# Cross-attention and mixture of experts: the order of the work between the last tanh and the first expert

## The reference

```
a    = x + xattn(layernorm(x), context)
       h   = tanh(text[t] + feature[f] + b)        for all 1024 x 77 pairs, 256 wide
       rho = h . w ; att = softmax(rho) ; text summed by att
       two tanh gates scale and shift the token
xn2  = layernorm(a)
prob = softmax(xn2 @ gate)                         8 experts
top  = the 512 of 4096 tokens with the largest prob, for each expert
out  = a + shared FFN(xn2) + scatter_add(top, prob * expert FFN(xn2[top]))
       FFN: 256 -> 1024, gelu, 1024 -> 256; each expert has weights of its own
```

## Time and profile before

| | |
|---|---|
| median of 3 runs | 893.86 us (893.48 to 893.88) |
| span of the profiled execution, first to last instruction | 892.1 us |
| TensorE busy | 801.3 us (90%) |
| ScalarE busy | 767.8 us (86%) |
| VectorE busy | 708.7 us (79%) |
| GpSimd busy | 307.6 us (34%) |

### The profile page before, as it was taken

The page is one execution under the profiler, slowest core; times in us unless marked ns, Lnnn a source line. Parts: engine busy times, 40 slices in busy tenths (PEclk is TensorE's granted clock), DMA queues, the critical chain, the costliest instruction groups (busy, mean ns, idle before and its releaser), DMA issues.

```text
span 892.1 us, 14125 instructions
## 1 busy us (share of the span) xinstructions
PE 801.3 (90%) x5385; PEld 472.7 (53%) x5385; DVE 708.7 (79%) x1405; ACT 767.8 (86%) x601; POOL 307.6 (34%) x537
## 2 busy tenths in 40 slices
PE   7975679569998999999999999999988999999996
PEld 5321123124443444445454455545766899999986
DVE  5899889898989689988878995894887877676641
ACT  3989999999999999999999999997753677676672
POOL 3310540615543007674002740052203145555424
PEclk9899999999999999999999999999999999999998
DMA  8000000000001000200000010002202365544513
GB/s 267 19 1 0 1 1 1 1 24 15 10 9 40 1 1 25 71 2 1 24 1 1 25 48 1 24 1 89 77 24 78 98 181 142 136 106 132 137 20 41
DMA packets 32406, 41.82 MB, mean 47 GB/s; under 512 B 2365, under 2 KB 29011, under 8 KB 32339
## 3 DMA queue, kind: packets, MB, share of 16 engines
q1 hardware_dynamic: 26083, 32.49, 10.9%
q0 software_dynamic: 6144, 8.39, 5.7%
q10 hardware_dynamic: 112, 0.04, 0.0%
HBM read 28.33 MB, written 12.58 MB: 46 GB/s over the span
## 4 chain that ended last, share of the span: by engine, by line
PE 39%; ACT 38%; issue 11%; DVE 9%; POOL 1%; DMA 0%; POOLq 0%; ACTq 0%; DVEq 0%
ACT z L995 31%; PE bank L914 10%; PE bank L937 9%; PE bank L787 7%; DVE z L1372 4%; PE bank L829 3%; PE bank L844 3%; ACT z L991 2%; ACT u L1038 2%; PE bank L763 2%; PE bank L715 1%; PE bank L952 1%; PE bank L817 1%; ACT L1038 1%; PE bank L888 1%
## 5 line engine op out<-in xcount | busy, mean ns | idle before, releaser
L995 ACT ACTIVATE z<-z 128x4096 f32<-128x4096 f32 (+5 forms) x157 | 520.9, 3364 | 4.6 <-DVE z L1372 4.4
L1372 DVE TENSOR_SCALAR z<-feat,txt_bias 128x1024 f32<-128x1024 f32 (+1 forms) x722 | 421.9, 656 | 36.5 <-PE bank L787 35.6
L787 PE MATMUL bank<-z,window 128*32 128x512 f32 x2464 | 304.9, 604 | 64.0 <-ACT z L995 62.5
L787 PEld LDWEIGHTS bank<-z,window 128*32 128x32 f32 x2464 | 70.0, 110 | 249.7 <-issue 134.1
L844 PE MATMUL bank<-ws_sb,u 128*128 128x256 f32 x512 | 126.3, 387 | 5.6 <-ACT u L1038 5.6
L844 PEld LDWEIGHTS bank<-ws_sb,u 128*128 128x128 f32 x512 | 92.2, 189 | 41.1 <-issue 19.8
L829 PE MATMUL bank<-tr,ws_s 128*128 128x512 f32 x384 | 107.9, 417 | 0.0
L914 PE MATMUL bank<-xg_s,w_s 128*128 128x512 f32 x384 | 99.5, 397 | 0.2 <-DVE xg_s L1672 0.2
L937 PEld LDWEIGHTS bank<-w_s,hid_s 128*128 128x128 f32 x672 | 86.3, 188 | 4.0
L937 PE MATMUL bank<-w_s,hid_s 128*128 128x256 f32 x672 | 88.2, 280 | 0.0
L1074 ACT ACTIVATE hid<-bank,vec 128x512 f32<-128x512 f32 x64 | 44.2, 690 | 49.3 <-PE bank L914 49.2
(11 more groups left out here) (264 smaller groups left out, 750.4 us busy)
## 6 DMA issues: line engine op xcount, KB each, us to landing
w_raw<-in_L_ffn_W_dram SPq DMA_DIRECT2D x16, 1024.0 KB, 5.6
x_ring<-in_x_dram SPq DMA_DIRECT2D x8, 512.0 KB, 7.9
xn_dram<-xn SPq DMA_DIRECT2D x8, 512.0 KB, 2.9
out_dram<-x_ring SPq DMA_DIRECT2D x8, 512.0 KB, 3.2
u<-in_L_ffn_Ws_dram SPq DMA_DIRECT2D x1, 1024.0 KB, 11.0
ws_sb<-in_L_ffn_Ws_dram SPq DMA_DIRECT2D x1, 1024.0 KB, 13.7
xg<-xn_dram,idx POOLq DMA_INDIRECT x32, 4.1
out_dram<-y,idx POOLq DMA_INDIRECT x32, 3.9
```

What stands on the lines that cost most here:

```text
L787: ins = e.matmul(sums[v][32 * r:32 * r + 32, :], window[:, c, 31 - k:63 - k], z[:, n % ZB, at_piece:at_piece + TOK], start=(v, r) not in b ...
L995: e.activation(part, part, ACT.Tanh).then_inc(signal(*step), 1)
L1372: ins = e.tensor_scalar(z[:, n % ZB, i * width:(i + 1) * width], feat_of(units, c), bias_of(units, t, c), None, ALU.add)
```

## The change

- **Sums ahead of FFN pieces.** In the last three blocks, `down` steps are taken out of the order and put behind the sums (`behind`), down(5,6) in two halves: the first behind `rho_out(7)`, the second behind `att_exp(7)`. Each of the last three blocks is summed by itself.
- **A gelu moved.** Of the four held gelus of unit 6, the first now stands ahead of `weigh(7)`, two behind the gates, and the fourth behind `logits_exp(7)`. `down_end(5,0)` moves to where `down_end(5,1)` was; `down_end(5,1)` and `store_out(5)` go behind the router.
- **The pieces' order and numbers.** down(6,0) and down(6,1) are interleaved so that bank 4 is used first; the two `down_end(6)` become two separate pieces.
- **First weights split on GpSimd.** A new step `split_first` does the copy and the subtract of each of the eight pieces on GpSimd, ahead of `masks` in its queue, behind `whole(7)`, which now stands in test 0. `split_hi` and `split_lo` of expert 0 go. The waits on them (`load_w1(1)`, `load_w2(1)`, `e_up`, `e_down`) turn to the new step.
- **VectorE idle in the first gathers.** `mark(1)` waits until gather 1 of the first four has landed (`FIRST_IN = 1`).
- **Around the first expert.** `mark_slots(1,3)`, `list(1,3)`, `fold(1)`, `folded(1)` and `gather(1)` come behind the turns of expert 0's rows, among its first steps; four filler pieces stand behind the turns.
- **Other banks.** Expert 0's gathered rows are turned into banks 0 and 1, and no more into 6 and 7.

The waits and banks of the steps follow in the code of each engine (`split_last`, `turned_bank`), which is left out here.

```diff
@@ -31,7 +31,7 @@
 AHEAD = 3
-TOGETHER, TOGETHER_FROM = 2, 93
+TOGETHER, TOGETHER_FROM, ALONE = 2, 93, 3
 BUSY = (20, 3, 5)
...
@@ -52,15 +52,17 @@
-TAIL_FILL = (7, 3)
-GELUS_BEFORE = 1
-TEST_FILL = (4, 4, 6, 4, 7, 3, 5, 5, 2, 3)
+TAIL_FILL = (4, 3)
+GELUS_BEFORE, GELUS_AFTER = 1, 3
+TEST_FILL = (5, 5, 6, 5, 7, 3, 5, 5, 3, 3)
 RANK_FILL = (1, 3, 6, 4)
-EXPERT_FILL = (23, 4, 0)
-SECOND_FILL = (8, 3, 2, 2, 9)
+SECOND_FILL = (8, 3, 3, 3)
+TURN_FILL = 2
 LIST_FILL = (0, 1, 0, 0)
 LAST_END = 1
+FIRST_IN = 1
+SPLIT_EARLY = 5
...
@@ -178,7 +180,7 @@
-            parts = (0, J // 2, J) if v == va - 1 and m == M - 1 else (0, J)
+            parts = (0, J // 2, J) if v == va - 1 and m >= M - 2 else (0, J)
             at_slots(n, FFN_PLACES, [[("up", v, m, 0, passes)], [("gelu", v, m)],
...
@@ -201,10 +203,14 @@
         summed.append(("rho", n))
-        if n < TOGETHER_FROM or n % TOGETHER == TOGETHER - 1 or n in unit_ends:
+        if LAST - ALONE <= n < LAST - 1:
+            steps = slots.pop(n, [])
+            behind += [step for step in steps if step[0] == "down"]
+            order += [step for step in steps if step[0] != "down"]
+        if n < TOGETHER_FROM or n >= LAST - ALONE or n % TOGETHER == TOGETHER - 1 or n in unit_ends:
             order += summed
             summed.clear()
-        if n < LAST - 1:
+        if n < LAST - ALONE:
             order += slots.pop(n, [])
...
@@ -224,12 +230,15 @@
-    lead = [step for steps in filler for step in steps]
-    filler = [piece for m in range(4) for piece in up(va, m)] + down(va, 0) + down(va, 1) + up(va, 4) + up(va, 5)
+    lead = behind + [step for steps in filler for step in steps]
+    filler = [piece for m in range(4) for piece in up(va, m)] + down(va, 0)[:2] + down(va, 1)[:2] + up(va, 4) + down(va, 0)[2:3]
+    filler += up(va, 5) + down(va, 0)[3:] + down(va, 1)[2:]
     for m in range(2, M):
     last_ffn = up(vb, 0) + [piece for m in range(1, M) for piece in up(vb, m) + down(vb, m - 1)] + down(vb, M - 1)
-    filler += last_ffn[:ENDS_BEHIND] + [down_ends(va)] + last_ffn[ENDS_BEHIND:]
+    ends = down_ends(va)
+    filler += last_ffn[:ENDS_BEHIND] + [ends[:1]] + last_ffn[ENDS_BEHIND + 2:ENDS_BEHIND + 4]
+    filler += last_ffn[ENDS_BEHIND:ENDS_BEHIND + 1] + [ends[1:]] + last_ffn[ENDS_BEHIND + 1:ENDS_BEHIND + 2] + last_ffn[ENDS_BEHIND + 4:]
...
@@ -244,18 +253,19 @@
-    first_split = [("split_hi", name, 0, h) for name in ("w1", "w2") for h in range(PIECES[0])]
+    first_split = [("split_first", name, h) for name in ("w1", "w2") for h in range(PIECES[0])]
     late = {step[1:3] for step in held}
-    order += [("logits_exp", va), ("router", va), *end[0], *(step for step in lead if step[0] == "up"), *end[1],
-              ("load_w1", 0), ("load_w2", 0), *end[2], ("att_exp", vb)]
-    order += [step for step in lead if step[0] == "down" and step[1:3] not in late]
+    downs = [step for step in lead if step[0] == "down" and step[1:3] not in late]
+    order += [("logits_exp", va), ("router", va), *end[0], *(step for step in lead if step[0] == "up"), downs.pop(0), *end[1],
+              ("load_w1", 0), ("load_w2", 0), *end[2], ("att_exp", vb), *downs]
     fill_chain(8)
     ends = [step for step in lead if step[0] in BY_VECTOR]
-    order += [*ends[:1], *held[:GELUS_BEFORE], *end[4], *end[5], *ends[1:], *end[6], *held[GELUS_BEFORE:]]
+    order += [*held[:GELUS_BEFORE], *end[4], *end[5], *ends[:1], *end[6], *held[GELUS_BEFORE:GELUS_AFTER]]
+    order += [*end[7], *end[9], *end[8], ("logits_exp", vb), *held[GELUS_AFTER:], ("y_shift_last", vb), ("router", vb),
+              ("values", NT - 2 * J, NT), *ends[1:]]
     held.clear()
-    order += [*end[7], *end[9], *end[8], ("logits_exp", vb), ("y_shift_last", vb), ("router", vb), ("values", NT - 2 * J, NT)]
     order += [step for step in lead if step[0] == "down" and step[1:3] in late]
...
@@ -270,7 +280,7 @@
         if k == 0:
-            order += reversed(end[10])
+            order += [*reversed(end[10]), *end[13], *first_split[:SPLIT_EARLY]]
         held.clear()
...
@@ -278,32 +288,25 @@
         order += steps
-    order += end[13]
-    high, low = [*first_split], [("split_lo", *step[1:]) for step in first_split]
+    order += first_split[SPLIT_EARLY:]
     fill(RANK_FILL[0])
-    order += [("masks",), high.pop(0), ("ranks",), ("rank_total",)]
+    order += [("masks",), ("ranks",), ("rank_total",)]
     fill(RANK_FILL[1])
-    order += [("offsets",), high.pop(0), ("ranked",)]
-    order.append(("slots_turn",))
+    order += [("offsets",), ("ranked",), ("slots_turn",)]
     fill(RANK_FILL[2])
-    order += [("slots",), high.pop(0)]
-    order.append(("mark", 0))
+    order += [("slots",), ("mark", 0)]
     fill(RANK_FILL[3])
     for q in range(4):
-        order += [("mark_slots", 0, q), ("list", 0, q), high.pop(0)]
+        order += [("mark_slots", 0, q), ("list", 0, q)]
         if q == 3:
         fill(LIST_FILL[q])
-    order += [*high, ("fold", 0), ("folded", 0), ("gather", 0)]
-    order += low[:PIECES[0]]
+    order += [("fold", 0), ("folded", 0), ("gather", 0)]
     fill(SECOND_FILL[0])
     order.append(("mark", 1))
-    for q in range(4):
+    for q in range(3):
         order += [("mark_slots", 1, q), ("list", 1, q)]
-        if q == 3:
-            order.append(("listed", 1))
         fill(SECOND_FILL[1 + q])
-    order += [("fold", 1), ("folded", 1), ("gather", 1)]
...
@@ -341,14 +344,14 @@
-    fill(max(0, len(filler) - sum(EXPERT_FILL)))
-    order += [*turn_gathered(0), *low[PIECES[0]:], ("load_w1", 1), ("load_w2", 1)]
-    for m in range(LAG):
+    order += [*turn_gathered(0), ("mark_slots", 1, 3), ("load_w1", 1), ("load_w2", 1)]
+    fill(TURN_FILL)
+    order += [("list", 1, 3), ("listed", 1), ("e_up", 0, 0), ("fold", 1), *up(0, 0)[1:3], ("folded", 1), ("gather", 1), *up(0, 0)[3:]]
+    for m in range(1, LAG):
         order += up(0, m)
+    fill(len(filler))
     for ex in range(E - 1):
         for m in range(M):
-            if ex == 0 and m < len(EXPERT_FILL):
-                fill(EXPERT_FILL[m])
             ahead = m + LAG
...
@@ -551,6 +554,9 @@
+        def turned_bank(ex, c):
+            return (MISC if ex else RHO)[c]
+
         EMPTIES = {
...
@@ -633,6 +639,9 @@
             return last_s[:, m - HC] if ex == E - 1 and m >= HC else hid_s[:, m % HC]
+
+        def split_last(name, ex):
+            return done("split_lo", name, ex, PIECES[1] - 1) if ex else done("split_first", name, PIECES[0] - 1)
...
@@ -1247,6 +1256,13 @@
                                     ALU.subtract).then_inc(signal(*step), 1)
+                elif kind == "split_first":
+                    name, h = args
+                    raw, parts = halves(name, 0, h)
+                    e.wait_ge(loaded[f"{name}_0"], 16)
+                    link(e.tensor_copy(parts[0], raw))
+                    e.wait_ge(pool_link, linked)
+                    e.tensor_tensor(parts[1], raw, parts[0].bitcast(F32), ALU.subtract).then_inc(signal(*step), 1)
                 elif kind == "gather":
...
@@ -1626,6 +1642,8 @@
                     ex, = args
+                    if ex == 1:
+                        e.wait_ge(first_gathered[FIRST_IN], 16)
                     link(e.tensor_tensor(in_tile[:], slot_a[:, :, ex:ex + 1].broadcast_to([P, NT, A]),
```

More of the change, by code:

```diff
@@ L190, in add @@
         order.append(("add", n))
-    summed, unit_ends = [], {*ends_at.values()}
+    summed, unit_ends, behind = [], {*ends_at.values()}, []
     for n in range(AHEAD - 1):
@@ L560, in xattn_moe_kernel @@
             "offsets": lambda: TOTAL, "slots": lambda: MISC[0], "listed": lambda ex: LIST,
-            "folded": lambda ex: SLOTS, "g_lo": lambda ex, c: MISC[c], "e_gelu": lambda ex, m: UP[m % 2],
+            "folded": lambda ex: SLOTS, "g_lo": lambda ex, c: turned_bank(ex, c), "e_gelu": lambda ex, m: UP[m % 2],
         }
@@ L685, in _ @@
                     else:
-                        e.wait_ge(*done("split_lo", "w1", ex - 1, PIECES[ex > 1] - 1))
+                        e.wait_ge(*split_last("w1", ex - 1))
                     if ex == 1:
@@ L693, in _ @@
                     if ex > 0:
-                        e.wait_ge(*done("split_lo", "w2", ex - 1, PIECES[ex > 1] - 1))
+                        e.wait_ge(*split_last("w2", ex - 1))
                     e.dma_start(w2_raw[:], W2[ex].rearrange("(m p) d -> p m d", p=P)).then_inc(loaded[f"w2_{ex}"], 16)
@@ L902, in _ @@
                             e.wait_ge(first_gathered[a], 16)
-                    turn_four(take(MISC[c]), xg[:, ex % 2], c).then_inc(signal(*step), 1)
+                    turn_four(take(turned_bank(ex, c)), xg[:, ex % 2], c).then_inc(signal(*step), 1)
                 elif kind == "e_up":
@@ L907, in _ @@
                     if m == 0:
-                        e.wait_ge(*done("split_lo", "w1", ex, PIECES[ex > 0] - 1))
+                        e.wait_ge(*split_last("w1", ex))
                     dst = take(UP[m % 2])
@@ L921, in _ @@
                     if m == 0:
```

(8 more changed lines are left out.)

## The result

The changed kernel takes 902.7 us (median of 4 runs, 900.99 to 902.83) against 893.85. The ratio, estimated over all executions, is 1.0095 [1.008, 1.0109]; the quotient of the medians is 1.0099. It is slower by 8.85 us. The forecast was 898.8, range 891 to 903: right in direction, 3.9 us too low, and inside the range by only 0.3 us. The 896.5 to 902 that the prediction gave its main forecast was missed.

What follows compares the result with a forecast made beforehand. It took TensorE's solid expert stream and the serial chain ahead of it, with 7.4 us of TensorE idle, as the bound. Terms -1.3 + 0 + 3.5 + 0 + 2.7 = +4.9 gave an 897.0 span, 898.8 us median; range 891 to 903.

Steps and rivals of the forecast that it cites:

- main forecast: Whole kernel: 898.8 us, its own range 896.5 to 902; chance 0.50.
- Head, -1.3: Last tanh to first test: sums and exp come earlier, -1.3 us (bounds -1.6, 0).
- Splits on GpSimd, +3.5: Tests 1 to 4: small two-input VectorE instructions wait for GpSimd's split instructions, +3.5 us (bounds 0, +9).
- rival "load": Rival in f_long's own forecast: GpSimd being busy costs, whatever its instruction length; same 902.7 us within 1; no chance given.
- Rival 1: Tests: port wait is small, GpSimd near its low ends, small instructions slip between; 895.9 us; chance 0.18.
- rival 3: Tests: paced at GpSimd's high ends, +9 us instead of +3.5, 904 us; chance 0.07.
- Gathers, +2.7: First gather to expert stream: TensorE gaps of 3.6 us before list(1,0), 1.7 before list(1,3); +2.7 us (+0.5, +4).
- Rival 2: Gathers: relief of VectorE decides, if second gather lands under G+2.0 (G: first gather's start); 891.5 us; chance 0.25.
- Tests without the splits, 0: Tests: table load leaves test 1 but TensorE is the limit there, fuller fills fit; 0 us (bounds -1, +1).
- Ranks, 0: Masks to first gather: VectorE's chain is not edited and GpSimd finishes splitting early; 0 us.

Runs made afterwards that it cites:

- a_back: The changed kernel with expert 0's eight weight pieces split on ScalarE and VectorE again, at the earlier places; 901.06 us, ratio to before 1.0079.
- f_long: The changed kernel with the same split work in four pairs of 128x1024, half as many and twice as long instructions; 905.51 us, ratio to before 1.0118.
- c_markfirst: The changed kernel with mark_slots(1,3) and list(1,3) ahead of the turns of expert 0's rows; 900.47 us, ratio to before 1.0069.
- e_splitonly: The kernel before with only the eight pieces' splits moved to GpSimd, behind whole(7); 898.01 us, ratio to before 1.0032.
- b_nowait: The changed kernel without mark(1)'s wait on the second gather; 898.42 us, ratio to before 1.0046.
- d_head: The change's head and new piece order alone, turns in the new banks; splits, lists and gathers as in the kernel before; 894.78 us, ratio 1.0009.
- g_order: The head-only kernel (d_head) with the last quarter of down(6,0) moved ahead of up(6,5) again; 892.86 us, ratio to before 0.9991.

## Why the prediction was right or wrong

**Head, -1.3: right** (-1.54, in every kernel that has it). The exp ran at 628.36 once the +1.65 is taken off, in place of 629.50.

**Splits on GpSimd, +3.5: right** in size (+3.16 and +3.63) and in mechanism, the size with some luck. The copy took 0.61 us and the subtract 1.27 (0.8 and 1.25 had been taken), a pair 1.91 with the gap and not 2.2. Tests 2 and 3 take 3.83 us each, two pairs to a hundredth: such a test lasts four GpSimd instructions, as argued from the earlier trace rows. But with the measured pair the prediction's own working gives 8 x 1.91 - 12.9 = +2.4, less what slips into gaps; its pair was too long, and where it took off for gaps the runs show more than the plain sum. Against a_back, test 1 bears 1.45 us of the price, tests 2 and 3 together 1.81, and test 4 nothing. f_long excludes the rival "load". Rival 1 (a small port wait) and rival 3 (+9) are out.

**Gathers, +2.7: near in sum** (+3.15), off in a part. List(1,0) and the turns came as forecast (turn G+12.4 for G+12.1). The gap ahead of list(1,0) was 2.0 us and not 3.6: the pieces in front of it ran until G+4.8 and not G+3.3, because the clock stood at its lower level, 1.2 GHz, for 3.4 us from 679.7 (0.53 over 679.6 to 683.2). Where the clock didn't fall ahead of the list, in c_markfirst, the gap is 3.38. The other gap was 1.93 for 1.7. Rival 2 (relief of VectorE decides) failed at the point it named: mark(1), which waits for the second gather to land, started at G+4.3, far above G+2.0. It was the wait that stood against the relief: in e_splitonly and b_nowait, which have the relief without the wait, list(1,0) comes behind no gap. How much of the term the wait is, stays open: b_nowait's profile shows 0.56 us, under a second clock fall.

**Tests without the splits, 0: wrong, the step that failed.** It is +2.24 (a_back; d_head 2.26). The step read test 1 for its table load and for TensorE's pieces, and found TensorE the limit. It passed over the reordered pieces: interleaving down(6,0) and down(6,1) keeps a slot of u taken, the gelu waits for it, and the sign counts wait behind the gelu in ScalarE's queue. The prediction checked the fills' number and not their order. g_order shows the mechanism.

**Not foreseen, +1.65 ahead of the last tanh.** No step of the change touches the first 600 us: the list of work is the same up to `down(5,6)`. The delay is there already at 52 us. Four profiles have a clock fall from about 34.4 to 38 us: after, b_nowait, f_long and g_order. In all four the tanh that stands at 50.7 to 51.1 us in the others starts at 52.4 to 52.5, and the last tanh ends at 616.9 to 617.0. The seven without that fall, before among them, end it at 615.1 to 615.6, with the same order of work up to there. Before and after, ScalarE's timeline:

```profile
50.74 3.62 ACT L995 ACTIVATE z<-z 128x4096 f32<-128x4096 f32 x1 [1.49 <-DVE z L1372]
```

```profile
52.46 3.62 ACT L1004 ACTIVATE z<-z 128x4096 f32<-128x4096 f32 x1 [2.94 <-DVE z L1388]
```

So it goes with one clock fall and not with the change; that the fall causes it fits the order in time, but wasn't tested by itself. Three of after's four executions are 902.6 to 902.8, one 900.99. Executions of before that ran beside the experiments lie at 892.9 to 894.8 and, the rest of them, at 896.0 to 896.2. Why after's drew the later tanh in the profile, and perhaps three times in four, stays open.

**Ranks, 0: right** (+0.1).

The terms add up: -1.54 + 2.24 + 3.16 + 0.1 + 3.15 + 0.1 = +7.2, and +1.65 makes the 8.9 of the spans. The forecast had +4.9; the failed step's 2.24 is about the 2.3 that lack, while the misses of head (-0.24), splits (-0.34) and gathers (+0.45) nearly cancel. The 3.16 and the 2.24 hold in this order of undoing, splits first. They overlap: e_splitonly gives the splits 3.63 and leaves 1.77 to the reordering.

## What to carry to other kernels

Work handed to GpSimd isn't free for VectorE just because VectorE's big instructions keep their time (the counts kept 0.47 us). A chain of tiny instructions with two SBUF inputs can be paced by the length of each GpSimd instruction beside it. So put such work beside a stretch with no such chain; instructions twice as long cost more here, and shorter ones weren't tried. When filler pieces are reordered, follow the buffer each one frees to the first instruction that waits for it, and count what is queued behind that one. A wait that makes a DMA issue faster pays only if someone waits for that DMA. And before a stretch of one profile is compared with another's, look whether the clock fell in one of them: here falls hid gains of 1 us and more.

## What the runs showed of the hardware

- The length of a 128x7 instruction on VectorE went from 0.23 us to 1.31 beside a GpSimd instruction of 1.27, and to 2.41 beside one of 2.37. The Trainium skill, "SBUF — State Buffer", section "Who interferes with whom", has the rule (whoever issues first holds the shared pair for the whole instruction). After and f_long agree that the wait lasts the whole instruction; who issued first their rows don't show, since the two are listed within 0.03 us of each other.
- An indirect gather's issue on GpSimd takes 0.95 us beside an idle VectorE (the third of after) and up to 1.93 beside its TENSOR_TENSOR of 128x1024 bf16 (the third of b_nowait). The same section of the Trainium skill infers that such an instruction leaves descriptor generation alone; these runs show otherwise for this one. The 128x640 TENSOR_TENSOR beside b_nowait's first gather changed nothing: 1.22 us, as in after.
- The granted clock fell to its lower level for about 3.5 us at a time in the windows shown, and for some 7 us at a time in places of the first 62 us. In after the fall at 679.7 came behind the first lists, short matmuls with idle gaps of 0.17 to 0.84 us between them. The kernel before and g_order have the same lists and show no fall there; the other profiles have one to three. A fall inside a gap costs nothing by itself (after's hid 1.4 us of list(1,0)'s gap, 2.00 against 3.38 in c_markfirst); over work it costs (eight down matmuls of e_splitonly took 2.77 us, 1.89 in g_order). What makes it fall in one execution and not in the next stays open.
